# Attention scores over 64 rows: keys packed two heads to a tile, a side ring of eight heads, and SyncE's loads of batch 0 in another order

## The reference

```python
q = (x @ Wq + bq).reshape(B, S, N_HEAD, HEAD_DIM).transpose(0, 2, 1, 3)
k = (x @ Wk + bk).reshape(B, S, N_HEAD, HEAD_DIM).transpose(0, 2, 1, 3)
v = (x @ Wv + bv).reshape(B, S, N_HEAD, HEAD_DIM).transpose(0, 2, 1, 3)
scores = jnp.einsum('bhqd,bhkd->bhqk', q / math.sqrt(HEAD_DIM), k)
scores = scores + attention_bias
scores = jnp.where(src_mask, -jnp.inf, scores.astype(jnp.float32))
probs = jax.nn.softmax(scores, axis=-1).astype(v.dtype)
ctx = jnp.einsum('bhqk,bhkd->bhqd', probs, v)
```

## Time and profile before

| | us |
|---|---|
| median of 3 runs | 852.12 |
| lowest, highest | 849.15, 852.52 |
| the profiled execution | 850.75 |
| its span, first to last instruction | 849.0 |
| PE busy | 813.2 (96%) |
| DVE busy | 737.0 (87%) |
| ScalarE busy | 622.9 (73%) |
| POOL busy | 163.3 (19%) |

### The profile page before, as it was taken

How to read it: one execution, slowest core, us unless ns; L and a number is a source line. 1 busy time by engine, 2 the same in 40 slices (tenths; PEclk the granted TensorE clock), 3 DMA queues, 4 the chain that set the end, 5 groups by cost and what they waited for, 6 DMA issues and landing times.

```text
span 849.0 us, 18721 instructions
## 1 busy us (share of the span) xinstructions
PE 813.2 (96%) x6029; PEld 697.4 (82%) x6029; DVE 737.0 (87%) x2472; ACT 622.9 (73%) x1286; POOL 163.3 (19%) x160
## 2 busy tenths in 40 slices
PE   8788899999999999999999999999999999999985
PEld 5665688889888888888888888988888888887874
DVE  7767767989989898998989898998989899878777
ACT  5257787978787887878788797878788787677551
POOL 2210122220402112120312222040211222111020
PEclk9889999999999999999999999999999999999998
DMA  7979786685756677676758878676768867475110
GB/s 226 202 205 220 163 203 157 157 200 139 171 161 172 166 160 189 164 184 142 188 155 178 166 161 198 143 173 157 177 158 176 177 166 181 114 174 143 51 32 25
DMA packets 147626, 137.33 MB, mean 162 GB/s; under 512 B 19314, under 2 KB 144819, under 8 KB 147524
## 3 DMA queue, kind: packets, MB, share of 16 engines
q1 hardware_dynamic: 145668, 134.99, 66.1%
q10 hardware_dynamic: 1856, 1.07, 0.8%
HBM read 98.23 MB, written 4.23 MB: 121 GB/s over the span
## 4 chain that ended last, share of the span: by engine, by line
PE 85%; DVE 7%; issue 2%; DMA 2%; ACT 2%; ACTq 1%; POOL 1%; POOLq 0%; DVEq 0%
PE turn_bank L1429 13%; PE back_bank L1473 12%; PE context_bank L1483 7%; PE score_bank L1686 7%; PE score_bank L1687 6%; PE front_bank L1467 5%; PE attend_bank L1467 5%; PE back_bank L1467 5%; PE back_bank L1453 3%; PE back_bank L1444 3%; PE attend_bank L1453 3%; PE front_bank L1522 3%; PE front_bank L1802 3%; PE attend_bank L1401 2%; DMA ks<-kl 2%
## 5 line engine op out<-in xcount | busy, mean ns | idle before, releaser
L594 ACT ACTIVATE sc<-sc,negmax 128x256 f32<-128x256 f32 x512 | 231.7, 505 | 20.0 <-DVE negmax L1290 18.6
L1290 DVE CUSTOM_DVE_ANT_0 sc<-score_bank,side 128x256 f32<-128x256 f32 x512 | 195.4, 420 | 35.6 <-PE score_bank L1687 26.4
L588 ACT ACTIVATE pt<-turn_bank 128x512 f32<-128x512 f32 x178 | 107.2, 603 | 126.4 <-PE turn_bank L1429 105.4
L1429 PE MATMUL turn_bank<-ident,sc 128*128 128x128 f32 x1024 | 157.1, 277 | 1.8 <-ACT sc L594 1.7
L1429 PEld LDWEIGHTS turn_bank<-ident,sc 128*128 128x128 f32 x1024 | 123.5, 142 | 32.5 <-issue 13.7
L1686 PE MATMUL score_bank<-ks,qs 128*128 128x256 f32 x512 | 122.9, 322 | 4.4 <-DMA ks<-kl 3.6
L1473 PE MATMUL back_bank<-w,ffT 128*128 128x256 f32 x480 | 111.1, 379 | 0.0
L508 POOL TENSOR_TENSOR rstd<-var,half_neg 128x2 f32<-128x2 f32 x64 | 50.9, 795 | 274.5 <-DVE var L1014 266.8
L1687 PE MATMUL score_bank<-mask_neg,ident_r 128*128 128x512 f32 x256 | 102.3, 400 | 0.0
L1473 PEld LDWEIGHTS back_bank<-w,ffT 128*128 128x128 f32 x480 | 90.9, 190 | 11.8
L1686 PEld LDWEIGHTS score_bank<-ks,qs 128*128 128x128 f32 x512 | 78.6, 193 | 13.0 <-issue 6.6
(11 more groups left out here) (298 smaller groups left out, 1974.7 us busy)
## 6 DMA issues: line engine op xcount, KB each, us to landing
side<-in_side SPq DMA_DIRECT2D x128, 512.0 KB, 5.7
qs<-qh SPq DMA_DIRECT2D x128, 64.0 KB, 4.4
qs<-ql SPq DMA_DIRECT2D x128, 64.0 KB, 4.5
ks<-kh SPq DMA_DIRECT2D x120, 64.0 KB, 4.2
ks<-kl SPq DMA_DIRECT2D x120, 64.0 KB, 4.5
wb<-in_wb SPq DMA_DIRECT2D x15, 512.0 KB, 7.3
xN<-in_x SPq DMA_DIRECT2D x16, 256.0 KB, 5.3
wc<-in_wc SPq DMA_DIRECT2D x16, 256.0 KB, 2.9
```

Source lines behind the costliest of these rows:

```text
L588: e.activation(pt[:, h % NP2, :, :], two(tbank[h % 2]), ACT.Copy).then_inc(copied[h % 4], 1)
L594: i = e.activation(sc[:, h % NS, q, :], sc[:, h % NS, q, :], ACT.Exp, bias=negmax[:, q, h:h + 1], scale=-1.0)
L1290: i = e.tensor_tensor_reduce(sc[:, s % NS, q, :], two(sbank[s % 2])[:, q, :], side[:, (H * X.i + s) % NSIDE, q, :], -1.0, 3.4e38, ALU.add, ...
L1429: i = e.transpose(tbank[h % 2][:, k * S + q * P:k * S + q * P + P], sc[:, h % NS, q, k * P:k * P + P], ident[:, :])
```

## The change

- `ks` becomes a tile of 8 pairs like `qs`: the even head of a pair in rows 0 to 63, the odd one in rows 64 to 127. `pack_k` writes four consecutive pairs instead of every second head. The zeros and their two memsets go, and with them the semaphore value `KS_SET`.
- The two score matmuls of a head contract over 64 rows, 0 to 63 for an even head and 64 to 127 for an odd one. The mask matmul behind them still contracts over 128 rows. Instructions and their order on PE are the same.
- The side ring holds eight heads; pair c + 3 is issued where pair c + 2 was, and in batch 0 slot 0 too issues one.
- On SyncE: grid A (two transfers) goes from slot 1 to slot 8 of turn -1; of the sixteen packs of heads 8 to 15 of batch 0 the eight with blocks 2 and 3 go from slot 9 of turn -1 to slot 3 of turn 0; `load_rows` goes from slot 3 to slot 13 of turn 0.

```diff
-NSIDE = 6
+NSIDE = 8
@@
-        ks = sb("ks", [P, H, S], F32R)
+        ks = sb("ks", [P, H // 2, S], F32R)
@@ pack_k
-            e.dma_start(ks[to, HM * m + u:HM * m + HM:2, :].bitcast(F32), k_[at, m, :].bitcast(F32)).then_inc(ld_stack[m], 16)
+            e.dma_start(ks[to, HU * m:HU * m + HU, :].bitcast(F32), k_[at, m, :].bitcast(F32)).then_inc(ld_stack[m], 16)
@@ load_early
-                load(ld_grid, (t_a[:, :, :], tall(d["grid_B"][0])), (t_b[:, :, :], tall(d["grid_B"][1])), (t_c[:, :, :], tall(d["grid_B"][2])),
-                     (x2[:, :, :], tall(d["grid_A"][0])), (x3[:, :, :], tall(d["grid_A"][1])))
+                load(ld_grid, (t_a[:, :, :], tall(d["grid_B"][0])), (t_b[:, :, :], tall(d["grid_B"][1])), (t_c[:, :, :], tall(d["grid_B"][2])))
                 e.wait_ge(act_set, ROWS_SET)
                 e.dma_start(d["ada_rows"], x3T[0:NB, :, :]).then_inc(st_ada, 16)
+
+            def load_grid_a():
+
+                load(ld_grid, (x2[:, :, :], tall(d["grid_A"][0])), (x3[:, :, :], tall(d["grid_A"][1])))
@@
-            later = {(-1, 1): load_early, (0, 3): load_rows, (0, 7): lambda: load_w2(0), (0, 11): lambda: load_w2(1), (0, 15): load_wa}
+            later = {(-1, 1): load_early, (-1, 8): load_grid_a, (0, 13): load_rows, (0, 7): lambda: load_w2(0), (0, 11): lambda: load_w2(1), (0, 15): load_wa}
@@ SyncE, body
-                    if s % 2 == 0 and X and (s < 12 or F):
+                    if s % 2 == 0 and X and (s < 10 or F):
 
                         c = s // 2
                         head(e, biased, X, 2 * c - 1)
-                        if not (t == 0 and s == 0):
-                            load_side(X if c < NPAIR - 2 else F, (c + 2) % NPAIR)
+                        load_side(X if c < NPAIR - 3 else F, (c + 3) % NPAIR)
@@
-                    if t == -1 and s == 9:
-                        e.wait_ge(ev["ql_ready"], F.n)
-                        e.wait_ge(ev["kl_ready"], F.n)
-                        e.wait_ge(pool_set, KS_SET)
-                        for b in range(NBLK):
-                            for u in range(2):
-                                pack_k(e, 1, b, u)
-                                pack_q(e, 1, b, u)
+                    for t0, s0, blocks_ in ((-1, 9, (0, 1)), (0, 3, (2, 3))):
+                        if is_step(t, s, t0, s0):
+                            e.wait_ge(ev["ql_ready"], 1)
+                            e.wait_ge(ev["kl_ready"], 1)
+                            for b in blocks_:
+                                for u in range(2):
+                                    pack_k(e, 1, b, u)
+                                    pack_q(e, 1, b, u)
@@ POOL, DVE
-            e.memset(ks[:, 0:HM, :].bitcast(F32), 0.0).then_inc(pool_set, 1)
-            e.memset(ks[:, HM:H, :].bitcast(F32), 0.0)
@@ PE, body
                         for q in range(TT):
-                            e.matmul(two(sbank[s % 2])[:, q, :], qs[:, s // 2, q * P:q * P + P], ks[:, s, :], start=(q == 0), stop=False)
+                            rows = slice(64 * (s % 2), 64 * (s % 2) + 64)
+                            e.matmul(two(sbank[s % 2])[:, q, :], qs[rows, s // 2, q * P:q * P + P], ks[rows, s // 2, :], start=(q == 0), stop=False)
```

More of the change, by code:

```diff
@@ L257, in build @@
         pool_set, dve_set, act_set, pe_set, st_ada = sem("pool_set"), sem("dve_set"), sem("act_set"), sem("pe_set"), sem("st_ada")
-        IDENT_SET, L0_SET, KS_SET, VP_SET = 3, 5, 6, 8
+        IDENT_SET, L0_SET, VP_SET = 3, 5, 7
         BANK_SET, IDS_SET, ARGS_SET, QUERY_SET, KEY_SET, QL0_SET, KL0_SET, PROJ_SET, BV_SET = 2, 3, 4, 5, 6, 7, 8, 9, 10
@@ L501, in set_values @@
                 e.memset(vp[:, :, :, :, :], 0.0).then_inc(pool_set, 1)
-                e.wait_ge(pool_set, 7)
+                e.wait_ge(pool_set, 6)
                 e.memset(vp[:, :, :, :, DH:DH + 1], 1.0).then_inc(pool_set, 1)
```

## The result

| | before | change |
|---|---|---|
| median, us | 852.32 | 939.5 |
| lowest, highest, us | 849.15, 853.12 | 938.75, 941.88 |
| span of the profiled execution, us | 849.0 | 937.6 |

The ratio is 1.1035, with a 95% interval of 1.1012 to 1.1058: the change is 87 us slower.

The account below looks back on a forecast made before the run. The prediction took PE to bound the steady part. It summed 850.75 + 99.4 (shape changes) - 1.5 - 6 (loads) - 3 (hidden work) = 939.7, so 940 us, with 908 to 960 us to hold 8 in 10.

Parts of the forecast that it names:

- What bounds the kernel: Steady part: PE is busy throughout, so an extra nanosecond on PE is an extra nanosecond of the kernel.
- The price of a head: Score matmuls on PE: two changes of array shape per head, 0.40 us together; 99.4 us added in all.
- Half price: Rival, score matmuls: array empties but weights load in the background, 0.18 to 0.20 us per head, 891 us; chance 0.07.
- free halves: Rival, score matmuls: 64 rows cost nothing extra, so the loads' gains win, 843 us; chance 0.06.
- What the rest moves: Loads, memsets, packs and ring, mainly around batch 0: 1.5 and 6 us gained, 3 us of added work hidden.
- Grid A: Start of batch 0: 0.5 MB less ahead of the key packs shortens PE's wait before the first score, 1.5 us gained.
- the side stall: Batch 0: DVE's idle on the side load before head 8, and PE's key-low wait behind it, go; 6 us gained.
- Hidden work: Batches 0 and 1: PE's idle time takes in part of its 12.8 us of added work, 3 us hidden.
- the full price's own range: Whole kernel, main case (chance 0.80): 929 us (0.37 us per head, all gains) to 952 us.
- Batch 0 gains nothing: Rival, batches 0 and 1: moved loads delay key packs or head 8, 7.5 us lost and 3 more, 953 us; chance 0.07.

Follow-up runs that it names:

- experiment 4: Full change with the mask matmul split in two, one half behind each score matmul: 1043.6 us; same split in the kernel before, over 128 rows: 853.05 us.
- The pairs: Full change, both heads of a pair scored in the even slot: 906.37 us (A, A, B, B), 905.09 us (A, B, A, B); kernel before, paired: 892.79 us.
- experiment 5: Full change with the mask matmul moved ahead of the two 64-row score matmuls: 942.91 us, ratio 1.1047.
- experiment 1: Kernel before with only the score matmuls cut to 64 rows; zeros, ring and loads as before: 940.08 us, ratio 1.1031.
- experiment 2: Kernel before with only SyncE's new order of loads; scores over 128 rows, ring of six heads: 851.38 us, ratio 0.9994.
- experiment 3: Kernel before with only the five setup loads (`load_rows`) moved from slot 3 to slot 9 of batch 0: 850.46 us, ratio 0.9988.

## Why the prediction was right, point by point

- **What bounds the kernel**: right. The steady period went from 48.4 to 54.3 us (54.6 forecast), with PE busy in all of it.
- **The price of a head**: right in mechanism and nearly in size. 0.386 us were measured where 0.40 us were booked. The parts lie a little differently: behind transposes the distance from the first to the second score was 0.20 us already before, as behind an exposed weight load, so the way in costs 0.17 us ahead of the first score and 0.02 us behind it. The way out costs 0.09 us in which no matmul starts and 0.10 us for the mask's exposed load. Behind context matmuls 0.20 us, as forecast. The term is 96.0 us instead of 99.4 us. Twice the changes gave twice the price (experiment 4), so the cost is per change and not per row or byte.
 The Trainium skill's "TensorEngine Tiling (Array Packing)", Key Properties, says that a change of mode drains TensorE, and its table of modes counts 64 rows as one. The runs agree in that each change costs time, 0.19 to 0.20 us, of which about half passes before the first matmul behind it starts; the trace shows the later start and not what fills the time ahead of it. The Trainium skill's "TensorE: Matmul & The Clock Gate", Part 3, says that matmuls on different row groups run at the same time and start about 4 ns apart. The pairs agree, with 3 to 7 ns in most of them.
- **Half price and free halves**: both out. The mask's weight load starts with its matmul at 444.07 us, and in experiments 4 and 5 the distances behind each change hold a full exposed load.
- **What the rest moves** is the step that failed, though the total came out. Grid A was booked at 1.5 us and the side stall at 6 us. Together the loads gave nothing: on top of the 64 rows (experiment 1) the full change is no faster than without them, and alone, with the ring of six heads (experiment 2), they change nothing that can be measured. Two things went wrong. First, the stall and the added PE work were summed as if they were apart, while the one hides the other: with the scores 64 rows deep, head 8 comes late enough for the old order of loads. Second, the late packs were checked against head 8 alone. They also hold the q tiles, so ScalarE's next query-high and DVE's query-low wait for them, 3.95 and 4.09 us in experiment 2. In the full change this second fault is mostly covered too: query-high starts at 54.59 us behind the packs, but PE's own query projection ends only at 54.23 us. Grid A gained nothing that can be told: the first score starts at 36.6 to 38.6 us in the six traces with it moved (36.82 us in the full change) and at 36.3 to 39.1 us in the five with it unmoved (37.53 us before).
- **Hidden work** was booked at 3 us. Between the profiled executions the span grew by 88.6 us of the 96.0 us added, so 7.4 us did not arrive. Some 5 of them were hidden in batch 0. The rest is spread over the steady periods (5.9 instead of 6.0 us each) and the last two batches.
- **The total** came out at 939.5 us against 940 us because these misses cancel, and that is luck: 99.4 - 10.5 = 88.9 us was forecast, 96.0 - 7.4 = 88.6 us was measured. The price of the changes of shape is understood and makes up nearly all of the loss; the agreement to half a microsecond is not earned. The ends of the full price's own range, 929 and 952 us, are not worked out in the prediction: 0.37 us per head and the largest gains that it names (2.44, 6.3 and 3 us) give some 931 to 934 us.
- **Batch 0 gains nothing**: right that the loads gain nothing, but not for its reason. The setup loads in slot 13 do not hold up the keys of batch 1: PE waits 1.2 us for them when that batch starts, in the full change as before. Its 953 us are wrong, since it gave the added work no cover.

None of the versions tried is measurably faster than the kernel before. Of the two ways to pick one head, the zeros in an unpacked key tile are the cheaper one.

## What to carry to other kernels

A matmul over fewer rows between matmuls over all rows paid about 0.2 us at each border here (half of it with no matmul started, half for a weight load that nothing hides), more than the 0.12 us that a 256-column matmul takes; zeros in a full tile cost no PE time beside it. If rows are to be split, put many split matmuls together, and first see whether putting them together makes PE wait. Don't book a removed stall and hidden added work as separate terms: one is the cover of the other. The pairs show the same again, where the price disappears in pairs that wait anyway. And when a transfer is put off, look who may overwrite its source, not only who reads its target.

## What the runs showed of the hardware that was not expected

- Two matmuls on the two halves of the rows run side by side even when the program has them as A, A, B, B: four took 0.51 us, the starts in twos, mostly 3 to 7 ns apart. The rows of the trace do not name the head, so that each two are A and B is inferred from the distance; in the kernel before and in the full change the two scores of one head never start closer than 0.11 us.
- Even so, a lone pair of heads over 64 rows is 0.15 us dearer than over 128 rows: side by side saves less than the two changes of shape cost.
- The stretches at 1.2 GHz near the start are not the same from kernel to kernel, and are worth microseconds. Batch 1 had a granted clock of 1.00 before and in experiment 3, and 0.92 in experiment 2, for the same PE work (39.2, 39.3 and 41.7 us busy). A pause of PE does not decide it alone: before, idle times of 1.30 and 1.24 us that ended at 91.61 and 93.94 us left the clock at 1.00, while in the full change it fell to 0.50 at 94.0 us behind one of 1.30 us that ended at 92.85 us.
